# A metaformer block on one core: norm stage woven block into block, attention reductions over two heads, weights loaded in runs, map loops of three strips

## The reference, cut to what matters

```python
x = x + conv_ref(ln_c(x), ...)      # ln_c: mean and variance over the 96 channels, eps 1e-6
# conv_ref, on 16x16 windows at step 14 (19 x 19 per image), 4 heads, 16-wide q and k, 24-wide v:
y = layernorm(tok) ; q, k, v = y @ wq, y @ wk, y @ wv
tok = softmax(q @ k.T / 4) @ v @ wproj + tok      # windows are added back, overlaps halved
# then on the map:
y = gelu(layernorm(tok2) @ fc1_w + fc1_b)          # 192 channels
y = y + gelu(depthwise 5x5 conv(y) + dw_b)
tok2 = y @ fc2_w + fc2_b + tok2
# after the residual, per pixel, in quantized steps (float8 e5m2 factors, float16 results):
t = t + linear(relu(linear(ln_t(t), W1, b1)), W2, b2)   # 96 -> 384 -> 96
```

## Time and profile before

| | us |
|---|---|
| median of 3 runs | 8934.74 |
| the profiled execution | 8930.41 |
| its span, first to last instruction | 8928.4 |

### The profile page before, as it was taken

How to read it: one execution, slowest core, us unless ns; L and a number is a source line. 1 busy time by engine, 2 the same in 40 slices (tenths; PEclk the granted TensorE clock), 3 DMA queues, 4 the chain that set the end, 5 groups by cost and what they waited for, 6 DMA issues and landing times.

```text
span 8928.4 us, 208174 instructions
## 1 busy us (share of the span) xinstructions
PE 7920.3 (89%) x76932; PEld 4796.9 (54%) x76932; DVE 5165.9 (58%) x9929; ACT 4663.7 (52%) x8702; POOL 2158.8 (24%) x1712
## 2 busy tenths in 40 slices
PE   7777799999999999999588989989989899899898
PEld 3333355455555555555366666666666666666665
DVE  5655677777777777777434444444444444444444
ACT  2222466666666666666255555545545555455554
POOL 0000334343434343434111111111211111112111
PEclk8888899999999999999699999999999999999999
DMA  4443344444444444444511111111111111111110
GB/s 113 120 119 105 89 98 97 98 97 98 97 98 97 100 95 101 95 103 96 58 37 41 35 41 41 39 41 35 45 41 35 41 39 41 41 35 45 41 35 24
DMA packets 480770, 612.23 MB, mean 69 GB/s; under 512 B 173262, under 2 KB 415696, under 8 KB 455316
## 3 DMA queue, kind: packets, MB, share of 16 engines
q1 hardware_dynamic: 480260, 605.46, 28.3%
HBM read 395.81 MB, written 166.64 MB: 63 GB/s over the span
## 4 chain that ended last, share of the span: by engine, by line
PE 29%; DVE 9%; ACT 8%; issue 5%; SPq 1%; DVEq 0%; ACTq 0%; DMA 0%; POOLq 0%; POOL 0%
PE P L1284 6%; PE P L1150 5%; PE P L1297 5%; PE P L1205 4%; ACT H L1357 4%; DVE H L1521 3%; PE P L1158 3%; DVE H L1514 2%; PE P L1313 2%; DVE Z L1536 2%; PE P L1124 1%; ACT Z L1382 1%; ACT L1382 1%; ACT L1345 1%; SPq L990 1%
## 5 line engine op out<-in xcount | busy, mean ns | idle before, releaser
L812 DVE TENSOR_REDUCE NM<-P 128x2 f32<-128x512 f32 x2888 | 1857.9, 685 | 564.2 <-PE P L645 558.9
L759 ACT ACTIVATE PROB<-P 128x512 f32<-128x512 f32 x2888 | 1491.1, 603 | 992.0 <-PE P L660 992.0
L1205 PE MATMUL P<-FC,XN 97*126 97x192 f32 x5408 | 1100.8, 342 | 15.7 <-ACT Y L1367 14.8
L1205 PEld LDWEIGHTS P<-FC,XN 97*126 97x126 f32 x5408 | 943.5, 196 | 168.4 <-issue 78.5
L660 PE MATMUL P<-QF,KS 32*128 32x256 f32 x11552 | 834.2, 403 | 90.8 <-DVE QF L806 90.3
L496 POOL TENSOR_TENSOR Y<-XHS,RNS 96x512 f32<-96x512 f32 x304 | 599.2, 1997 | 1226.9 <-DMA RNS<-rnorm 932.7
L660 PEld LDWEIGHTS P<-QF,KS 32*128 32x128 f32 x11552 | 525.3, 185 | 615.1 <-DVE QF L806 544.1
L1351 ACT ACTIVATE SQ<-Z 96x512 f32<-96x512 f32 x260 | 163.8, 630 | 1286.7 <-DVE Z L1501 1286.7
L668 PE MATMUL P<-PROB,V 128*32 128x256 f32 x11552 | 775.8, 386 | 1.5 <-ACT PROB L759 1.5
L1367 ACT ACTIVATE Y<-P 126x384 f32<-126x384 f32 x1352 | 705.6, 570 | 109.9 <-PE P L1205 104.3
L1091 POOL TENSOR_TENSOR T<-T,Y 96x512 f16 (+1 forms) x260 | 299.3, 1151 | 1723.3 <-DVE Y L1525 1723.3
(11 more groups left out here) (141 smaller groups left out, 12134.5 us busy)
## 6 DMA issues: line engine op xcount, KB each, us to landing
RBC<-sums SPq DMA_DIRECT2D x456, 160.0 KB, 3.1
X<-x2map SPq DMA_DIRECT2D x52, 1344.0 KB, 8.3
XHS<-xhat SPq DMA_DIRECT2D x76, 768.0 KB, 6.2
RNS<-rnorm SPq DMA_DIRECT2D x38, 1536.0 KB, 9.3
x2map<-XHS SPq DMA_DIRECT2D x76, 768.0 KB
T<-in_x SPq DMA_DIRECT2D x52, 960.0 KB
out<-T SPq DMA_DIRECT2D x52, 960.0 KB, 4.9
X<-in_x SPq DMA_DIRECT2D x32, 1536.0 KB, 13.2
```

The costliest lines, as they stand in the source:

```text
L759: A.activation(PROB[:, par, u, :], P[:, B_ST[u], :], ACT.Exp, scale=DQ ** -0.5).then_inc(act_exp, 1)
L812: V_.tensor_reduce(NM[:, :, 32 * u + DQ], P[:, B_S[u], :].rearrange("p (a m) -> p a m", a=2), axis=AX.X, op=ALU.max).then_inc(dve_max, 1)
L1205: m = M.matmul(P[0:KW, 5 + (r + 2) % 3, i * MLP:(i + 1) * MLP], xnf[:, RI * WX * w:RI * WX * w + KW], FC1[:, :], start=True, stop=True)
```

## The change

It has four parts.

1. **Norm stage.** The centred values come straight from one matmul with the matrix I - 1/96 (CENW, made once on VectorE). ScalarE copies them out of PSUM into XH and squares them out of PSUM. VectorE no longer centres; it multiplies into new buffers XO, which are what SyncE stores. The squares are summed by four matmuls of 32 weight columns side by side (as the map stage does), then copied (VS) and gathered by one matmul with REP. TensorE's program of block i now carries the spreading of block i-1 in pieces between the pieces of block i. The loads of weights are smaller and five instead of three.
2. **Attention stage.** `row_max` is two instructions over two heads each, the exponential two instructions over two heads each. The waits count accordingly; `maxima` now waits for the first exponential instruction of the window before, which covers heads 0 and 1 instead of head 0 alone.
3. **Weights of the map stage.** The depthwise weights, W1 and W2 are loaded row by row and turned over by eight TensorE transposes into PSUM; VectorE copies them out. W_LOADS is 20.
4. **Loops of the map stage.** On TensorE, ScalarE and VectorE the loop is 17 rounds of 3 strips. The place in T is a constant.

```diff
 (norm stage, sync)
+            def fetch(par, i): ... sp.dma_start(X[par] ...).then_inc(x_loaded[par], 16)
+            def keep(par, i):
+                hold(sp, sp_passed, dve_xh, i * 8 + 8)
+                sp.dma_start(xhat[...], XO[par][:, :]).then_inc(stored[par], 16)
+                hold(sp, sp_passed, dve_rn, i + 1)
+                sp.dma_start(rv[...], RCP[0:NCH, 1, :]).then_inc(r_stored, 16)
+            with sp.Fori(0, nblk // 2 - 2) as k:
+                for par in range(2):
+                    i = k * 2 + par
+                    hold(sp, sp_passed, pe_cen, i * 8 + 16)
+                    fetch(1 - par, i + 3)
+                    keep(par, i)
 (tensor)
+            def spread(i, j):
+                if j == 0: pe.wait_ge(dve_parts, i + 1)
+                if j >= 2: pe.wait_ge(dve_xh, i * 8 + (j - 1))
+                for c in (2 * j, 2 * j + 1):
+                    m = T.matmul(P[0:C, B_BC + j % 2, ...], BSEL[:, c, :], RB[:, :], start=True, stop=True)
+                m.then_inc(pe_bc, 1)
+            def body(par, i, k):
+                pe.wait_ge(x_loaded[par], k * 16 + 16)
+                def centred(j):
+                    T.matmul(P[0:C, j % 4, :], CENW[:, :], X[par][:, pair(j)], start=True, stop=True).then_inc(pe_cen, 1)
+                def variance(q):
+                    pe.wait_ge(act_sq, i * 8 + (2 * q + 2))
+                    for g in range(4):
+                        c = 4 * q + g
+                        m = T.matmul(P[32 * g:32 * g + 32, B_VAR, 0:CW], SSEL[:, NV - 1 - c:NV - 1 - c + 32],
+                                     SQ[:, c // 2 % 4, ...], start=(q == 0), stop=(q == 3))
+                    m.then_inc(pe_var, 1)
+                for j in range(4):
+                    centred(j)
+                for q in range(4):
+                    variance(q)
+                    if q < 2:
+                        centred(4 + 2 * q)
+                        centred(5 + 2 * q)
+                    if not first(i, 1):
+                        spread(i - 1, 2 * q)
+                        spread(i - 1, 2 * q + 1)
+                pe.wait_ge(act_vs, i + 1)
+                T.matmul(P[0:C, B_STAT, 0:CW], REP[:, :], VS[:, :], start=True, stop=True).then_inc(pe_rep, 1)
 (scalar)
+                for j in range(8):
+                    act.wait_ge(pe_cen, i * 8 + (j + 1))
+                    A.activation(XH[par][:, pair(j)], P[0:C, j % 4, :], ACT.Copy)
+                    if j >= 4: act.wait_ge(pe_var, i * 4 + (j // 2 - 1))
+                    A.activation(SQ[:, j % 4, :], P[0:C, j % 4, :], ACT.Square).then_inc(act_sq, 1)
+                    if j == 3 and not first(i, 1): second_std(i - 1)
+                act.wait_ge(pe_var, i * 4 + 4)
+                A.activation(VS[:, :], P[:, B_VAR, 0:CW], ACT.Copy).then_inc(act_vs, 1)
+                act.wait_ge(pe_rep, i + 1)
+                A.activation(STD[:, 0, :], P[0:C, B_STAT, 0:CW], ACT.Sqrt, bias=EPS[:, 0:1]).then_inc(act_std, 1)
 (vector, block i: the chain of small steps as before, then)
+                for j in range(8):
+                    dve.wait_ge(pe_bc, i * 8 + (j + 1))
+                    V.tensor_tensor(XO[par][:, pair(j)], XH[par][:, pair(j)], P[0:C, B_BC + j % 2, :], ALU.mult).then_inc(dve_xh, 1)
+                dve.wait_ge(act_std2, i + 1)
+                V.reciprocal(RCP[:, 1, :], STD[:, 1, :]).then_inc(dve_rn, 1)
 (attention stage)
-                        pe.wait_ge(act_exp, n(s, 4 * NPOS, 4 * j - 3))
+                        pe.wait_ge(act_exp, n(s, 2 * NPOS, 2 * j - 1))
                     maxima()
-                    for u in range(4):
-                        A.activation(PROB[:, par, u, :], P[:, B_ST[u], :], ACT.Exp, ...)
+                    for u in (0, 2):
+                        A.activation(PROB[:, par, u:u + 2, :], P[:, B_ST[u]:B_ST[u] + 2, :], ACT.Exp, ...)
-                for u in range(4):
-                    V_.tensor_reduce(NM[:, :, 32 * u + DQ], P[:, B_S[u], :]..., axis=AX.X, op=ALU.max)
+                for i in range(2):
+                    V_.tensor_reduce(NM[...][:, 2 * i:2 * i + 2, :, DQ], P[:, B_S[0]:B_S[0] + 2, :]..., axis=AX.X, op=ALU.max)
 (map stage)
-                load(DW[0:25, :], dww.rearrange("c a y x -> (a y x) c"))
-                load(W1R, w1.rearrange("n k -> k n"))
-                for f in range(3):
-                    load(W2R[:, f, :], w2[:, f * 128:(f + 1) * 128].rearrange("n k -> k n"))
+            load(DWN, dww.rearrange("(h c) a y x -> c h (a y x)", h=2))
+            load(W1N, w1.rearrange("(f n) k -> n f k", f=3))
+            load(W2N, w2)
+            for f in range(3):
+                M.transpose(P[0:C, f, 0:128], W1N[:, f, :], IDN[:, :])
+                M.transpose(P[:, 3 + f, 0:C], W2N[:, f * 128:(f + 1) * 128], IDN[0:C, 0:C])
+            for h in range(2):
+                t = M.transpose(P[0:25, 6, h * C:(h + 1) * C], DWN[:, h, :], IDN[0:C, 0:C])
+            t.then_inc(pe_turn, 1)
+            pe.wait_ge(dve_step, 1)
-            with pe.Fori(0, nstrip - 1) as u:
-                v = pe.snap(u + 1)
-                first_half(...)
-                second_half(v, ..., half_of(pe, u), v)
+            with pe.Fori(0, (nstrip - 1) // ROUND) as k:
+                for s in range(ROUND):                      # ROUND = 3
+                    u = pe.snap(k * ROUND + s)
+                    v = pe.snap(u + 1)
+                    first_half(...)
+                    second_half(v, ..., s * TO, v)
 (the same on scalar and vector)
```

More of the change, by code:

```diff
@@ L44, in norm_stage @@
         XH = [sb(f"XH{i}", [C, TOK]) for i in range(2)]
+        XO = [sb(f"XO{i}", [C, TOK]) for i in range(2)]
         SQ = sb("SQ", [C, 4, 2 * CW])
-        STD = sb("STD", [C, CW])
+        VS = sb("VSA", [128, CW])
+        STD = sb("STD", [C, 2, CW])
         VR = sb("VR", [C, CW])
@@ L110, in _ @@
+                    fetch(1 - par, i + 3)
+                    keep(par, i)
+            for i in range(nblk - 4, nblk):
+                if i + 3 < nblk:
+                    sp.wait_ge(pe_cen, i * 8 + 16)
+                    fetch((i + 3) % 2, i + 3)
+                keep(i % 2, i)
             sp.wait_ge(r_stored, 16 * nblk)
             for par in range(2):
-                sp.wait_ge(stored[par], 16 * (nblk // 2 + par))
-        def pipeline(eng, front, back):
-            front(0, 0, None)
+                sp.wait_ge(stored[par], 16 * (nblk // 2))
@@ L117, in pipeline, with blocks @@
+        def blocks(eng, body):
+            body(0, 0, 0)
+            body(1, 1, 0)
             with eng.Fori(0, nblk // 2 - 1) as k:
                 i = eng.snap(k * 2)
-                front(1, i + 1, k)
-                back(0, i)
-                front(0, i + 2, k + 1)
-                back(1, i + 1)
-            front(1, nblk - 1, nblk // 2 - 1)
-            back(0, nblk - 2)
-            back(1, nblk - 1)
+                body(0, i + 2, k + 1)
+                body(1, i + 3, k + 1)
+        first = lambda i, upto: isinstance(i, int) and i < upto
@@ L151, in back @@
[L151 to L160 removed]
+            def spread(i, j):
+                if j == 0:
+                    pe.wait_ge(dve_parts, i + 1)
+                if j >= 2:
+                    pe.wait_ge(dve_xh, i * 8 + (j - 1))
+                for c in (2 * j, 2 * j + 1):
+                    m = T.matmul(P[0:C, B_BC + j % 2, (c % 2) * CW:(c % 2 + 1) * CW], BSEL[:, c, :], RB[:, :], start=True, stop=True)
+                m.then_inc(pe_bc, 1)
@@ L162, in _ @@
+            blocks(pe, body)
+            for j in range(8):
+                spread(nblk - 1, j)
         @block.scalar
@@ L184, in _, with body @@
             V.memset(EPS[:, 1:2], 1e-5)
-            dve.wait_ge(w_loaded, 48)
+            dve.wait_ge(w_loaded, 80)
+            V.tensor_tensor(CENW[:, :], CENW[:, :], MEANW[:, :], ALU.subtract)
             V.tensor_copy(BSEL[:, :, :], BSEL32[:, :, :]).then_inc(dve_init, 1)
-            def centre(par, i):
-                for j in range(8):
-                    dve.wait_ge(pe_mean, i * 8 + (j + 1))
-                    V.tensor_tensor(XH[par][:, pair(j)], X[par][:, pair(j)], P[0:C, j % 4, :], ALU.subtract).then_inc(dve_cen, 1)
-            def chain(par, i):
+            def body(par, i, k):
                 v0 = i * VSTEPS
```

213 lines of the change are left out of this document (86 added, 127 removed).

## The result

| | us |
|---|---|
| before, median of 4 runs beside the runs after | 8932.75 (8927.77 to 8935.31) |
| after, median of 4 runs | 8670.24 (8663.2 to 8676.6) |
| ratio | 0.9707, interval 0.969 to 0.9723 |
| span of the profiled execution after | 8664.5, granted clock 0.949 |
| predicted | 8529 (8430 to 8640) |

A forecast was written before the change was run, and what follows sets the result against it. TensorE's own time nearly bounds attention and map, a chain of waits the norm stage. Norm -400, attention -40, weights -48, loops +82 make -406 from 8930.4: 8524, as a median 8529 us; range 8470 to 8590, wider 8430 to 8640.

The forecast's parts named there:

- A jump is 3.1 idle and some 2 of slow clock, 5.1: Map stage: each of 16 jumps back costs TensorE 5.1 us, +82 us in all; bounds 0 and +96.
- rival 2: Norm stage: the loop is slower than its sum, 17.0 us a block, 8609 us in all; 18 in 100.
- Code streaming: Map stage: three strips' code, 327 KB, isn't kept but streams in, with a 3 us wait every third strip.
- rival 1: Map stage: the longer code is kept after all, or fetched ahead of the jump; 8447 us; 13 in 100.
- rival 3: Map stage: code cannot be streamed as fast as used, slower than before, 9600 us at 3.1 a block; 2 in 100.
- ScalarE's and VectorE's bodies grow too, but their stalls would fall into TensorE's: Map loops: the longer code of these two engines adds no cost beyond TensorE's own stalls.
- What they remove is register work ... It is worth nothing: Map loops of three strips: saving register work for the place in T gains nothing where TensorE runs without a gap.
- Norm stage: Norm stage: a block takes 14.5 us instead of 27.3, bounds 13.0 and 17.0; -400 us together.
- the chain of 14.1: Norm stage: the new loop's dependent steps, sum 13.2 us, with five hand-overs of 0.18 make 14.1 a block.
- the 15.2 us: Norm stage: block time if its 3.15 MB moved at the skill's 207 GB/s; 22 us less gain; not adopted.
- Attention: Attention stage: merged maxima save 0.12 us a window, 19 or 87 us by windows counted; -40 taken, bounds +40 and -87.
- Weights: Start of map stage: loading weights by whole rows saves about 54 us, transposes and copies add 6; -48, bounds -54 and -30.

The follow-up runs named there:

- e3: e1, with TensorE waiting ahead of each strip's first product (fc1) for GpSimd's last addition of the strip before; 9133.35 us, ratio 1.0222.
- h3: e1, with TensorE waiting ahead of the convolution in each strip for one small addition of an idle GpSimd; 8639.59 us, ratio 0.9671.
- g1: The changed kernel with ScalarE's and VectorE's map loops back at one strip a round, only TensorE's at three; 8667.96 us, ratio 0.971.
- f4: e2, with the attention loop's 36 strips also unrolled into one round; 8375.64 us, ratio 0.9388.
- e4: The changed kernel with TensorE's three-strip map loop turned to begin, and jump, ahead of the convolution; 8674.2 us, ratio 0.9709.
- f3: The changed kernel with TensorE's and VectorE's map loops back at one strip a round, only ScalarE's at three; 8545.99 us, ratio 0.9578.
- e1: The changed kernel with the map loops of TensorE, ScalarE and VectorE back at one strip a round; 8445.71 us, ratio 0.9453.
- e2: The changed kernel with all 51 strips of the map loops unrolled into one round, no jump back; 8423.11 us, ratio 0.9429.
- h2: The changed kernel with TensorE's and ScalarE's map loops back at one strip a round, only VectorE's at three; 8417.41 us, ratio 0.9428.
- h1: f4, with the norm stage's second reciprocal moved behind the next block's second multiplication and two buffers for the second root; 8342.07 us, ratio 0.9342.
- g3: f4, with the attention row maxima back to four instructions of one head each; 8411.13 us, ratio 0.9416.
- f1: e4, with ScalarE's and VectorE's map loops at one strip a round, so only TensorE has three; 8528.84 us, ratio 0.9557.

## Why the prediction was wrong, step by step

**The step that failed** is "A jump is 3.1 idle and some 2 of slow clock, 5.1", used for the map stage with the upper bound "+96 (6 us each)". That jumps back would stall TensorE, and that nothing would cover it, was right, and the 3.1 idle was exact (46.1 / 15). The term that was mis-sized is the slow clock: a jump cost 14.0 in all, so some 10.9 of slow clock instead of 2. I had taken the 2 from the product after a jump of the attention loop, where other work follows, and gave the bound by the same rows; no row of before has a stall at z1. e3 and h3 show that the place decides, g1 that TensorE's loop alone brings all of it, and the traces that the clock came back only in the convolution. A hint was in the earlier trace rows: the norm stage, whose TensorE waits in every block, had a granted clock of 0.87, and I used that only for rival 2. Why the clock doesn't rise within z1 stays open. The 5.1 was a fair reading of the windows next to a jump of the attention loop (5.3 longer than elsewhere in the profile before), but too little even there: some 8 by f4, so the price of a jump reaches beyond the windows beside it. In the profiles the map strips grew by 218 us for 82, which is 136 of the miss of 141; the norm stage came out 18 us better than forecast, attention and weights 24 us worse.

**Code streaming** was right: not kept (rival 1, 13%), streamed without cost between jumps (rival 3), a stall at z1 every third strip (L1301 after, L1284 before). "ScalarE's and VectorE's bodies grow too, but their stalls would fall into TensorE's" holds in the change, where g1 equals all three; but ScalarE's alone costs 100 us, so a cure on TensorE only (e4) bought nothing. ScalarE's code fetches 98 packets more in f3 than in e1, 0.8 MB.

**"What they remove is register work ... It is worth nothing"** is at least doubtful: e2 and h2 lie 23 and 28 us below e1. The loops of one strip took 4337 (e1) and 4340 us (before) in the map stage, h2 4320 and the unrolled kernels 4309 to 4336, so a gain would be of the size of the spread.

**Norm stage**, 14.5 us a block forecast and 13.82 measured, -418 for -400: the chain of 14.1 was close, TensorE's wait for the parts was 1.2 us instead of 2, and the clock was 0.98 where the earlier trace rows had 0.87, with gaps of 1.2 us a block in place of those before. The wait named as TensorE's remaining one is the right one: h1 removes it and gains 1.2 us a block. DMA didn't bind: h1 moves 251 GB/s in this stage, loads and stores together. The prediction misread the page on this. The Trainium skill, "DMA: Bandwidth & Descriptors", section "Latency and other measured facts", gives 207 GB/s for rows 512 KiB apart per direction, while the 15.2 us set the bytes of both directions against it. The stores alone, 1.57 MB a block, would take 7.6 us by that figure, an estimate that lies below every block time here, so no run here tests it.

**Attention**, -20 for -40: the instruction's size was right (1222 ns), the merge worth 25 to 29 by g3, and some of it was not seen in the change, whose five jumps were 0.8 us longer each than before. The 40 was a choice between 19 and 87, so a gain that lies near it is no proof of the count of windows behind it. By medians over the strips some windows stayed as they were (4.33 us for 4.33), as forecast, and many others became 0.06 to 0.13 us shorter.

**Weights**, -44 for -48: from the traces alone, not tried by itself.

## What to carry to other kernels

Price a stall of TensorE by what it has to do behind it: here 2 to 5 us of standing cost 3.8 to 14 us, by place, and 0.3 to 1.5 at a wait that existed. Look in the trace for the work at which the clock comes back, not only at the first matmuls behind the stall. Put a loop's jump, on every engine whose stall reaches TensorE, where such a wait is, or unroll: straight code streamed in for nothing. When a consumer is moved later, look for who waits to overwrite what it reads; that wait can cost more than the move saves.

## What was not expected of the hardware

- After a stall of 2.4 to 3.5 us ahead of z1 the granted clock stayed at 0.50 for 24 to 31 us, while TensorE was busy 10.00 of 10 us (change, g1, e3); after one of 2.1 us (h3), or two of 1.9 to 3.5 (f1), ahead of the convolution it was back after 3.4 to 10.2 us. In all 103 strips of these traces in which it fell at z1, it came back only in the convolution.
- The code of ScalarE and VectorE came on q14 in packets of 8.2 KB (350 packets, 2.87 MB in the change; 98 of them are there with ScalarE's three-strip body alone, f3, and 82 with VectorE's, h2, over the 170 of e1), TensorE's on q8 in 16.4 KB (665, 10.90 MB). ScalarE's jump had a stall of 2.0 to 2.3 us, VectorE's none.
- A jump ahead of the convolution has two stalls, the second behind 11 matmuls: 30 stalls in 15 jumps, 78.8 us of idle time in f1.
